# Four edits around the short stages of a two-layer transformer block: a ring of eight loads, attention outputs as token rows, later constants, and a bias product in two F32R passes

## The reference

```
part 1   qkv = x @ w_qkv; 16 heads of 16; softmax(q k^T / 16) v; out @ w_out
part 2   twice: zn = rmsnorm(z)*norm_w; two of four groups by softmax, in each the better of two experts;
         z = z + sum_e combine_e * (silu(zn @ w1_e^T) @ w2_e^T)
part 3   q, k, v with bias; causal attention with a position term per head; out @ o_w^T + o_b
part 4   scores = layernorm(x)*g+b @ centroids^T; expert e takes the 512 best tokens still free, for e = 0..7;
         routed + gelu(layernorm(routed)*g+b @ w1_e + b1_e) @ w2_e + b2_e
```

## Time and profile before

| | us |
|---|---|
| median of 3 timed runs | 3163.26 (3162.42 to 3168.05) |
| the profiled execution, its own time | 3172.95 |
| its span | 3171.2 |
| granted TensorE clock, mean over the span | 0.915 |

### The profile page before, as it was taken

How to read it: one execution, slowest core, us unless ns; L and a number is a source line. 1 busy time by engine, 2 the same in 40 slices (tenths; PEclk the granted TensorE clock), 3 DMA queues, 4 the chain that set the end, 5 groups by cost and what they waited for, 6 DMA issues and landing times. The chain is left out here.

```text
span 3171.2 us, 61217 instructions
## 1 busy us (share of the span) xinstructions
PE 2637.8 (83%) x16220; PEld 1567.0 (49%) x16221; DVE 1923.9 (61%) x4538; ACT 1598.1 (50%) x2506; POOL 1056.3 (33%) x1712
## 2 busy tenths in 40 slices
PE   8689999999997679975799885988888888648887
PEld 5333333333333568864688643444444444425554
DVE  3478888888884853336533383677677664756641
ACT  3267777777776643433434363566666654402212
POOL 1424111111111555543455463333222312403333
PEclk9699999999999879995799987999999996769999
DMA  4500101010102512215122193011111103603321
GB/s 168 192 21 14 27 14 27 14 27 14 27 7 64 161 40 67 69 60 148 37 69 68 59 297 121 22 27 27 27 27 27 27 11 108 228 21 106 102 82 63
DMA packets 267217, 215.30 MB, mean 68 GB/s; under 512 B 186365, under 2 KB 230913, under 8 KB 266308
## 3 DMA queue, kind: packets, MB, share of 16 engines
q1 hardware_dynamic: 236868, 136.40, 15.2%
q0 software_dynamic: 17728, 52.20, 5.2%
q10 hardware_dynamic: 12480, 25.17, 2.2%
HBM read 129.26 MB, written 85.72 MB: 68 GB/s over the span
## 5 line engine op out<-in xcount | busy, mean ns | idle before, releaser
L390 DVE TENSOR_REDUCE att_mparts<-att_S 128x2 f32<-128x1024 f32 x640 | 776.8, 1224 | 171.2 <-DVEq L386 169.2
L350 ACT ACTIVATE l_z<-att_S 128x1024 f32<-128x1024 f32 x512 | 517.6, 1024 | 213.8 <-ACTq L357 213.5
L266 PE MATMUL att_S<-att_qT,att_kT 64*128 64x512 f32 (+3 forms) x1792 | 431.7, 474 | 47.1 <-PEq L261 44.6
L254 PE MATMUL att_S<-att_kT,att_qT 64*128 64x512 f32 (+3 forms) x1792 | 391.6, 431 | 75.1 <-PEq L248 64.7
L350 ACT ACTIVATE att_room<-att_S 128x1024 f32<-128x1024 f32 (+3 forms) x384 | 318.5, 831 | 219.4 <-ACTq L357 216.6
L266 PEld LDWEIGHTS att_S<-att_qT,att_kT 64*128 64x128 f32 x1792 | 175.7, 185 | 475.4 <-issue 465.3
L254 PEld LDWEIGHTS att_S<-att_kT,att_qT 64*128 64x128 f32 x1792 | 188.7, 191 | 173.6 <-issue 167.2
L282 PE MATMUL att_OP<-l_z 128*32 128x512 f32 x2048 | 273.5, 606 | 0.9 <-PEq L276 0.7
L396 DVE CUSTOM_DVE_ANT_0 att_unused<-att_S,att_mask 128x128 f32<-128x128 f32 (+3 forms) x512 | 228.3, 488 | 74.2 <-DVEq L386 74.2
L183 POOL COPY l_z<-l_z 128x256 f32<-128x256 f32 x32 | 12.7, 398 | 632.0 <-POOLq L182 632.0
L1107 POOL DMA_INDIRECT experts_xs<-scaled,ffn_source x142 | 138.7, 976 | 193.4 <-PEq L1138 142.0
(11 more groups left out here) (311 smaller groups left out, 5135.3 us busy)
## 6 DMA issues: line engine op xcount, KB each, us to landing
qkv<-qkv_y ACTq DMA_DIRECT2D x32, 384.0 KB, 2.5
l_z<-qkv SPq DMA_DIRECT2D x48, 256.0 KB, 3.6
qkv<-qkv_y SPq DMA_DIRECT2D x32, 384.0 KB, 3.5
att_room<-qkv SPq DMA_DIRECT2D x48, 256.0 KB, 3.0
rows<-post_rows SPq DMA_DIRECT2D x32, 384.0 KB, 3.0
ffn_w<-in_w ACTq DMA_DIRECT2D x12, 1024.0 KB
ffn_w<-in_w SPq DMA_DIRECT2D x4, 2048.0 KB, 19.4
post_at<-ao SPq DMA_DIRECT2D x64, 128.0 KB, 2.9
```

The source lines that it names most:

```text
L254: mm=pe.matmul(S[:,b,h,at:at+n],qT[r,s,qt*128:qt*128+128],kT[r,s,half*512:half*512+n],start=True,stop=True)
L266: mm=pe.matmul(S[:,b,h,f:512],kT[r,s,kt*128:kt*128+128],qT[r,s,c*512+f:c*512+512],start=True,stop=not diag)
L350: nc.scalar.activation(pr[:,n%4,:,f:512],S[:,ring["e",n],:,f:512],ACT.Exp,scale=exp_scale).then_inc(s_free[ring["e",n]],1)
L390: nc.vector.tensor_reduce(mparts[:,s,:,2*qt+half],S[:,b,:,0:width(qt,half)],AX.X,ALU.max).then_inc(end,1)
```

## The change

1. `rms_logits`: the ring of row buffers has 8 places instead of 4.
2. `ao` is laid out as token rows of 256 columns. The attention store writes its 64 columns of each token at a stride of one row; the load of a tile in `attn_post` reads 128 whole rows.
3. Constants that are first used later get a semaphore of their own, `late_consts`. In `post1`, `gm`, `bm` and `proj` are issued behind the first two tiles' loads, PE waits for them before the first score product and DVE before the first `centred`. In `ffn1`, `ident`, `b1` and `b2` no longer hold back DVE and PE's counting; their place in SP's list is the same.
4. `post1`: DVE splits the bias row into a high part (F32R, rounded by the copy) and the rest, and PE adds the two parts as two F32R products with a row of ones; before it was one float32 product.

```diff
@@ -123,15 +123,15 @@
-                def store(bg):
+                def store(b,g):
...
-                    sp.dma_start(ao[bass.ds(bg,1)][0].rearrange("(t p) c -> p t c",p=128),aon[:].rearrange("p t h d -> p t (h d)")).then_inc(ao_stored,16)
+                    sp.dma_start(ao[bass.ds(b*SEQ,SEQ),64*g:64*g+64].rearrange("(t p) c -> p t c",p=128),aon[:].rearrange("p t h d -> p t (h d)")).then_inc(ao_stored,16)
...
-                    if not first: store(b*GROUPS+g-1)
+                    if not first: store(*((b,g-1) if g>0 else (b-1,GROUPS-1)))
@@ -143,7 +143,7 @@
-                store(BATCH*GROUPS-1)
+                store(BATCH-1,GROUPS-1)
@@ -640,8 +640,8 @@
-            ident=m.sb("ident",[128,128]); ones=m.sb("ones",[1,128]); bias=m.sb("bias",[1,DIM]); gm=m.sb("gm",[128,DIM]); bm=m.sb("bm",[128,DIM]); proj=m.sb("cent",[128,KC,EXPERTS])
-            rows=m.sb("rows",[128,RL,3,DIM]); COLS=EXPERTS; NCONST=16*6; SECOND=(1.0+LN_EPS,LN_EPS*LN_EPS)
+            ident=m.sb("ident",[128,128]); ones=m.sb("ones",[1,128],F32R); onesf=m.sb("onesf",[1,128]); bias=m.sb("bias",[1,DIM]); bias_parts=m.sb("bias_parts",[1,2,DIM],F32R); gm=m.sb("gm",[128,DIM]); bm=m.sb("bm",[128,DIM]); proj=m.sb("cent",[128,KC,EXPERTS])
+            rows=m.sb("rows",[128,RL,3,DIM]); COLS=EXPERTS; NCONST=16*3; SECOND=(1.0+LN_EPS,LN_EPS*LN_EPS)
@@ -654,19 +654,19 @@
                     sp.dma_start(ident[:],ident_d).then_inc(consts,16)
-                    for dst,s in ((gm,g_d),(bm,b_d)):
-                        sp.dma_start(dst[:],s.partition_broadcast(128)).then_inc(consts,16)
                     sp.dma_start(bias[:],bias_d.rearrange("(o d) -> o d",o=1)).then_inc(consts,16)
-                    sp.dma_start(proj[:],cent_d.rearrange("(k p) n -> p k n",p=128)).then_inc(consts,16)
                 KEEP=12 if last else 9
...
                     if new is not None:
-                        b,u=new//TILES,new%TILES
                         sp.wait_ge(a_free,1).then_inc(a_free,-1)
-                        sp.dma_start(at[:,new%RL].rearrange("p (g c) -> p g c",g=GROUPS),ao[b*GROUPS:b*GROUPS+GROUPS,u*128:u*128+128,:].rearrange("g p c -> p g c")).then_inc(a_loaded[new%RL],16)
+                        sp.dma_start(at[:,new%RL],tile_of(ao,new)).then_inc(a_loaded[new%RL],16)
                         sp.wait_ge(x_free,1).then_inc(x_free,-1)
                         sp.dma_start(xt[:,new%RL],tile_of(x_in,new)).then_inc(x_loaded[new%RL],16)
+                    if last and n==1:
+                        for dst,s in ((gm,g_d),(bm,b_d)):
+                            sp.dma_start(dst[:],s.partition_broadcast(128)).then_inc(late_consts,16)
+                        sp.dma_start(proj[:],cent_d.rearrange("(k p) n -> p k n",p=128)).then_inc(late_consts,16)
                     if x is not None and not last:
@@ -698,7 +698,7 @@
-                if last: pe.wait_ge(half_done,2)
+                if last: pe.wait_ge(half_done,4)
@@ -712,8 +712,10 @@
                             mm=pe.matmul(Y[:,p%RY,0:DIM],aT[:,p%2,128*c:128*c+128],w[:,c,:],start=c==0,stop=c==KC-1 and not last)
-                        if last: mm=pe.matmul(Y[:,p%RY,0:DIM],ones[:],bias[:],start=False,stop=True)
+                        if last:
+                            for part in range(2): mm=pe.matmul(Y[:,p%RY,0:DIM],ones[:],bias_parts[:,part],start=False,stop=part==1)
                         mm.then_inc(y_full,1)
+                    if last and s==0: pe.wait_ge(late_consts,48)
                     if s is not None:
@@ -755,9 +757,15 @@
                 if last:
-                    V.memset(ones[:],1.0).then_inc(half_done,1)
+                    V.memset(onesf[:],1.0).then_inc(dve_done,1)
+                    dve.wait_ge(dve_done,1)
+                    V.tensor_copy(ones[:],onesf[:]).then_inc(half_done,1)
                 dve.wait_ge(consts,NCONST)
-                issued=0; x_made=0; centred_made=[]
+                if last:
+                    V.tensor_copy(bias_parts[:,0],bias[:]).then_inc(dve_done,1)
+                    dve.wait_ge(dve_done,2)
+                    V.tensor_tensor(bias_parts[:,1],bias[:],bias_parts[:,0].bitcast(F32),ALU.subtract).then_inc(half_done,2)
+                issued=2 if last else 0; x_made=0; centred_made=[]
                 for n in range(2,NT+7):
@@ -801,6 +809,7 @@
+                    if last and x==0: dve.wait_ge(late_consts,48)
@@ -815,7 +824,7 @@
-        R=4; ZR=8
+        R=8; ZR=8
@@ -1418,9 +1427,9 @@
-                sp.dma_start(ident[:],ident_d).then_inc(consts,16)
-                sp.dma_start(b1[:],b1_d).then_inc(consts,16)
-                sp.dma_start(b2[:],b2_d.rearrange("(o d) -> o d",o=1)).then_inc(consts,16)
+                sp.dma_start(ident[:],ident_d).then_inc(late_consts,16)
+                sp.dma_start(b1[:],b1_d).then_inc(late_consts,16)
+                sp.dma_start(b2[:],b2_d.rearrange("(o d) -> o d",o=1)).then_inc(late_consts,16)
@@ -1429,9 +1438,10 @@
-                pe.wait_ge(consts,16*6)
+                pe.wait_ge(consts,16*3)
...
+                    if e==0: pe.wait_ge(late_consts,16*3)
@@ -1484,7 +1494,7 @@
-                act.wait_ge(consts,16*6)
+                act.wait_ge(late_consts,16*3)
@@ -1511,7 +1521,7 @@
-                dve.wait_ge(consts,16*6)
+                dve.wait_ge(consts,16*3)
@@ -1604,7 +1614,7 @@
-    qkv=scratch("qkv",TOK,3*DIM); ao=scratch("ao",BATCH*GROUPS,SEQ,4*HD)
+    qkv=scratch("qkv",TOK,3*DIM); ao=scratch("ao",TOK,DIM)
```

More of the change, by code:

```diff
@@ L634, in attn_post @@
         T=m.ps("T",[128,2,512]); Y=m.ps("Y",[128,RY,512]); T2=m.ps("T2",[128,2,512]); SC=m.ps("SC",[128,512])
-        consts=m.sem("consts"); half_done=m.sem("half_done"); pool_done=m.sem("pool_done"); dve_done=m.sem("dve_done")
+        consts=m.sem("consts"); late_consts=m.sem("late_consts"); half_done=m.sem("half_done"); pool_done=m.sem("pool_done"); dve_done=m.sem("dve_done")
         a_loaded=[m.sem(f"a_loaded{i}") for i in range(RL)]; x_loaded=[m.sem(f"x_loaded{i}") for i in range(RL)]; a_free=m.sem("a_free"); x_free=m.sem("x_free")
@@ L1374, in assigned_experts @@
         CN=m.ps("CN",[128,512]); RK=m.ps("RK",[128,512])
-        consts=m.sem("consts"); tri_ready=m.sem("tri_ready"); dve_done=m.sem("dve_done"); part_ready=m.sem("part_ready"); count_full=m.sem("count_full"); flags_ready=m.sem("flags_ready"); rank_full=m.sem("rank_full")
+        consts=m.sem("consts"); late_consts=m.sem("late_consts"); tri_ready=m.sem("tri_ready"); dve_done=m.sem("dve_done"); part_ready=m.sem("part_ready"); count_full=m.sem("count_full"); flags_ready=m.sem("flags_ready"); rank_full=m.sem("rank_full")
         hot_ready=m.sem("hot_ready"); table_full=m.sem("table_full"); table_ready=m.sem("table_ready"); token_loaded=[m.sem(f"token_loaded{e}") for e in range(EXPERTS)]
```

## The result

The changed kernel takes 3144.97 us (median of 6 runs, 3143.0 to 3154.48) against 3162.84 for the kernel before (6 runs, 3155.22 to 3168.05): a ratio of 0.9943 with a 95% interval of 0.9925 to 0.996, 18 us less (13 to 24). A second comparison, on another chip, gave 0.9944 (0.9928 to 0.9959). The profiled execution took 3143.0 us by its own time, span 3141.2, mean clock 0.922. It is the fastest of its six, while that of before (3172.95) lies above all six of its kernel, so the two traces differ by 30 us and the kernels by 18.

A forecast was written before the change was run, and what follows sets the result against it. It took the ring to bound `rms1`, PE `post1`, DVE and its input `post0`, and the sixth constant the start of `ffn1`. Terms of 24.9 us off 3163.26 gave 3138 us, eight in ten from 3126 to 3150.

The forecast's parts named there:

- Ring of eight: In `rms1`, eight buffers shorten the interval between scalings from 1.93 to 1.55 us: 10 us, bounds 3 and 16.
- three successors: Next bounds in `rms1` per tile: DVE's work 1.3 us, DMA engines 1.55, SP's list 1.4 to 1.6.
- Token rows: Larger pieces in the `post0` tile load shorten waits: 2.5 us, at most 5; the strided store costs nothing.
- Later constants in `post1`: The first tile's load is issued 2.6 us earlier in `post1`: 2.7 us gained, bounds 1.5 and 3.2.
- F32R at the full clock: In `post1`, PE's interval falls to 2.31 and DVE's 2.40 bounds: 21 intervals give 2.5 us.
- F32R at the low clock: In `post1`, cheaper bias products save 0.43 us a tile and the clock may rise earlier: 6 us.
- late end: Case for `post1` in which the clock rises where it did: 9 intervals x 0.43 = 3.9 us.
- `ffn1`, 1.2: DVE's first wait in `ffn1` ends with the third constant, not the sixth: 1.2 us, bounds 0.5 and 1.5.
- All waits fall away: Rival: `rms1` at DVE's 1.30 and the clock of `post1` rising at once, 11 us more, 3127; chance 0.17.
- Transfers bound `rms1`: Rival: interval stays at 1.80, ring gives 3 us, `post0` gains nothing; 3148; chance 0.16.
- The clock stays low through `post1`: Rival: clock at 1.2 GHz to the end of `post1`, 21 more slow intervals, 3171; chance 0.05.
- Stores dear: Rival: the strided attention store lands later and delays attention loads, 16 us lost, 3154; chance 0.05.

The follow-up runs named there:

- run 1: Changed kernel with the ring of the second normalisation back at 4 buffers; ratio to the kernel before 0.9978, 3160.06 us.
- run 8: Changed kernel with the stores of `rms1` 12 tiles behind their loads in place of 8, with 12 output buffers; 3136.8 us, ratio 0.9903.
- run 10: Changed kernel with 128-row F32R bias, `rms1` stores 12 tiles behind, first turn awaiting only `w` and `ident`, attention output by group; 3131.3 us, ratio 0.9882.
- run 11: Changed kernel with the constants of `post1` and `ffn1` early again, as before the change; 3150.7 us, ratio 0.9942.
- run 4: The kernel before, profiled again with no edit; 3165.18 us.
- run 2: Changed kernel with the bias as one float32 product from one row again, without the bias parts and their waits; 3144.38 us, ratio 0.9927.
- run 5: The kernel before with its float32 bias product in `post1` made over 128 rows, zeros below the bias; 3146.63 us in a single execution.
- runs 5 to 7: run 5, run 6, and the changed kernel with the bias as one F32R product over 128 rows, 3140.7 us in a single execution.
- runs 6, 7, 9, 10, 11: run 6, run 10, run 11; changed kernel with 128-row F32R bias, 3140.7 us; that plus later `rms1` stores and fewer waits before PE's first turn, 3131.09 us.
- run 6: Changed kernel with the bias product of `post1` left out; 3141.65 us in a single execution.

## Why the prediction was right, and where not

The time was forecast at 3138 us and the range at 3126 to 3150; it is 3145. The direction and the largest term were right, the sum of 24.9 was 7 too large, and one step failed. Only the ring's term can be checked against the time (run 1); the others are read at their place in the traces.

*Ring of eight, 10 us:* right. The mean of `rms1` over seven traces with eight buffers is 59.0 us, over four with four buffers 70.8: 11.8. The interval came at 1.44 in place of 1.55. Of the three successors that I named SP's list is the one (run 8); I took 1.55 from the transfers, so that it came near is in part luck; the estimate for the list itself was 1.4 to 1.6. That the figures of all three lay close together hid two errors. DVE's floor is 1.19, not 1.3, as the scaling overlaps with the additions. And the rate of 253 GB/s that I worked out by dividing by the busy share is no limit: with DVE full the stage's engines moved 338. The share of 0.89 was the strongest argument of the rivals on transfers, and it said nothing: it was as high at 280 GB/s.

*Token rows, 2.5 us:* too large. In traces where `post0` kept its clock, the stage has a mean of 92.0 us with token rows (five traces) and 93.1 by group (four): 1.1 us at its place, and nothing in the time (run 10). The landing shortened from 2.9 to 2.6 in the first two traces, but over all of them it is 2.8 to 2.9 by group and 2.5 to 2.8 with token rows; and DVE's own interval was already the bound in most tiles. The stores cost nothing that can be told: the means of the attention stages stand 1.6 us apart, in a scatter of 7 to 10.

*Later constants in `post1`, 2.7:* 1.5 by the first traces of the two kernels, 1.8 by run 11; the same kernel before had its first turn 0.7 sooner in run 4, so neither figure is firm. What I missed stands in the earlier trace rows and the code: PE's wait for `half_done` is ahead of the first turn, and two DVE instructions now hang on `bias` there, so that they, and not the tile, ended last. "About when the tile lands" was late: run 2, without the parts, has the first turn 0.76 us sooner.

*F32R at the full clock, 2.5:* 2.40 a tile with DVE full, as forecast. The 22 intervals behind the ninth (I had counted 21) take 53.4 us in place of 55.3: 1.9, since not every one of the changed kernel's is 2.40; two of them are 2.54 and 2.79.

*F32R at the low clock, 6:* this step failed. The part that is the product's own work was right: 3.05 against 3.04 forecast, 0.42 x 7 = 2.9 us for the seven slow tiles of the changed kernel's trace. The rest, the 2.1 above the late end's 3.9, for a clock that rises earlier because the one-row product is "halved and not gone", isn't there: with the float32 product the rise came at 32, 34 and 44 us, with two F32R passes at 30 to 48. The trace after showed what I had forecast (30 in place of 44; the first nine intervals 6.4 us shorter), and it was chance. Of the cause I had half: the kind of product is what counts, and not PE's busy time (run 5), but two passes over one row are still passes over one row. Two pairs of traces whose clock rose at about the same moment tell what F32R is worth in the stage as a whole, at both clocks: 4.2 us between run 2 and the changed kernel (rise at 32 and 30), 3.9 between the kernel before and run 11 (44 in both). Forecast were 8.5.

*`ffn1`, 1.2:* the cast came 1.1 earlier. What is left of it at the stage's end can't be told. Run 11 lasts 418.4 us in this stage, the two traces of the changed kernel 417.8 and 417.7, those of the kernel before 417.6 and 422.0; but traces with one and the same code here go from 413.9 (run 1) to 418.6 (run 10).

With what the runs gave, the sum is 11.8 + 1.1 + 1.8 + 1.9 + 2.9 = 19.5, beside a measured 18. The agreement proves little: the interval of the 18 goes from 13 to 24, and by the pairs above the last two terms together are 3.9 to 4.2 and not 4.8.

I wrote that I would be wrong if an untouched stage moved by more than 2 us. `att1` and `experts1` did, by 2.9 and 2.7. Run 4 shows both for the kernel before itself. The test was set below what one execution of a stage of 700 us tells from another.

*The rivals.* All waits fall away (3127): not by this change, but both of its halves exist, the one 12 tiles behind, the other with 128 rows, and together they gave 3131. Transfers bound `rms1`: refuted by the interval of 1.44 where the rival had 1.80, and by run 8. The clock stays low through `post1`: not seen in fourteen traces; its longest stay was 48 us. Stores dear: refuted by run 10.

The Trainium skill (TensorE: Matmul & The Clock Gate, Part 1) says that sustained matmul activity releases the low clock. In `post0` and in runs 5 to 7 the trace agrees, 8 to 10 us behind the stage's start; in `post1` with a one-row product in each tile it doesn't, at 4.00 busy us of 4, nor in `rms1` of run 8, at 12.00 of 12.

## What to carry to other kernels

Look for one-row products in a stretch in which PE is full and the granted clock stays at 0.50: filling the unused rows with zeros cost nothing in PE's time (at the full clock 0.59 us in run 5, with one row 0.69), and was worth more here (11 us and over in the stage) than making the product cheaper (about 4). Only one row against 128 was tried; attention has products over 64 rows at a granted clock of 1.00 (the changed kernel from 300 to 900 us). When a ring is deepened, see at once what the same queue issues between two loads: here the wait of a store held up the next load. And before a gain is put down to an edit, profile the kernel before a second time: one trace of a stage with a clock that rises by chance can tell 10 us that aren't there.

## What was not expected of the hardware

- With PE hardly pausing from its first turn on, the granted clock of `post1` stayed at 0.50 until 30 to 48 us behind the stage's start when each tile had a product over one row, and until 10 when that product went over 128 rows (run 5), at the same number of instructions. In `rms1` it stayed at 0.50 with PE at 12.00 busy us of 12 and no such product (run 8).
- The busy share of the DMA engines was 0.89 at 225 GB/s, 0.91 at 280 (after) and 1.01 at 338 (run 8): it isn't a measure of what is left.
- In five traces (runs 6, 7, 9, 10, 11) the clock of `post0` rose 10 us after the stage's start, fell back to 0.50 from about 17.5 to 24.3 us, and rose again. These are the five in which the stage began latest, 1005.1 us or more into the span; in the nine others it began at 1001.7 to 1004.7 and kept its clock. Their `post0` took 92.9 to 94.7 us, the others' 91.3 to 93.4. What all fourteen have is a pause of PE at that place: from 16 to 18 us into the stage PE works for 0.3 to 0.5 of 2 us. In the five the clock had risen at 10.5 to 10.8 us and fell 17.4 to 17.6 us into the stage, within that pause, 0.6 to 1.0 us after its start; in the nine others it had risen at 9.3 to 10.1 and stayed up. That the moment of the start or of the rise decides it is not shown; they only go along with it.

```profile
1023.53 2.04 PE L714 MATMUL post_Y<-post_w,post_aT 128*128 128x256 f32 x4 [1.70 <-PEq L712]
```

(The end of that pause in run 6, whose stage starts at 1005.3.)

- What sets the moment of the late rise in `post1` (30 to 48) stays open, beyond that it never came before the turns of the normalised tiles had joined.
